# A graph-attention kernel on one core: q fetched as 32-bit rows instead of three bf16 parts

## The chip, the cores and the metric

The kernel runs on one core of one Trainium2 chip, in one launch. The metric is the device time of the whole program in microseconds (us); lower is better. The engines are named as in the profile: PE (TensorE, with its weight loads as PEld), DVE (VectorE), ACT (ScalarE), POOL (GpSimd) and SP (SyncE, which here only issues DMAs). The engines run their own instruction lists and meet only at semaphores, which the kernel sets and waits for by hand.

## What is computed

Two layers of a typed graph transformer over 6250 nodes and 100000 edges (sorted by destination), then a linear layer and a layer norm. One layer, cut to what matters:

```python
k = typed_linear(x, ntype, Wk); q = typed_linear(x, ntype, Wq); v = typed_linear(x, ntype, Wv)   # 6250 x 128
kT = einsum('nhd,htdo->nhto', k, Watt);  vT = einsum('nhd,htdo->nhto', v, Wmsg)                  # per node, 32 edge types
kw = kT[src, :, etype];  m = vT[src, :, etype]                                                   # 100000 rows, 8 heads x 16
a = einsum('ehd,ehd->eh', kw, q[dst]) * pri[:, etype].T / SQRT_D
att = edge_softmax(a, dst, n)
hag = segment_sum(m * att[:, :, None], dst)
h = silu(typed_linear(hag, ntype, Wa)) * alpha + x * (1 - alpha);  h = layernorm(h) * g + b
```

## The kernel before, in words

Each layer has two stages. `fused(l)` projects q, k and v node tile by node tile, builds the table of all (node, edge type) rows (kT and vT side by side, 256 words) and stores it to DRAM; the q rows go to DRAM in node order. `attend(l)` then walks over the edges. After the second layer `finish()` does the last layer norms and the output.

In `attend` the edges are laid out in slots of 128 edges; all edges of a slot have their destination in one tile of 128 nodes. Four slots are a quad, 8 quads a block (32 slots), and 26 blocks a layer, so that there are 208 quads in a layer and 416 in all. Blocks 0 and 1 are written out, the others run in a loop of six blocks per turn. For each quad:

- POOL (`gather`, L790 to L798) issues four indirect DMAs (L796), each fetching 128 table rows into one slot of `rows`, a ring of three blocks (24 quads). From the 25th quad on it first waits until PE has summed the quad that had the place (`sum_psum`). Each of the DMAs counts up the semaphore `rows_in` of the quad.
- SP (`load_places`, L607) loads the places of the quad's edges in their node tile, broadcast to all partitions, in bf16.
- DVE (`turned`, L1755 to L1761) compares them with the partition's number: one instruction makes `onehotT`, 128 nodes x 512 edges, of ones and zeros. It runs two quads ahead.
- PE (`fetch_q`, L1272 to L1282) multiplies `onehotT` with the q rows of the slot's node tile, which puts q[dst] for 128 edges into PSUM. It runs one quad ahead. q lies in SBUF as three bf16 parts (`q_parts`, high, middle and low) whose sum is the 32-bit number, so there are three products per slot that add up in PSUM, 12 per quad. Before them PE waits for `onehotT_ready` and for `prod_ready` of the quad before the last.
- DVE (`multiply`, L1748) multiplies PSUM with the gathered k rows, after `rows_in` and `q_psum`; `head_sums` (L1763, the reduce in L1766) adds them up per head; `find_maxima` does, spread over the next block's quads, the softmax maxima of a block.
- DVE (`weigh`, L1770, with its multiplication in L1775) weighs the messages 12 quads later, PE (`sum_quad`, L1284, its products in L1293) sums them per node with a second one-hot that ACT makes (`mark`, L1010, lines L1015 and L1018), and DVE (`add`, L1784, L1790) adds the sums to `sums` in SBUF.

The products of `sum_quad` have 32-bit operands on both sides; each stands in the trace as two loads and two products, so 8 records per quad; each of them has 136 columns.

Ahead of the first quad of each layer stands a start-up. SP loads q from DRAM into the space of `sums` in four parts (L629). ACT copies the upper halves of the 32-bit words as bf16 (L1042), DVE subtracts them (L1907), ACT copies the rest, DVE subtracts again, ACT copies the last rest: 12 copies and 8 subtractions, chained by `q_copied` and `q_left`. Only then does DVE clear `sums` (L1910), make the first two `onehotT`, and PE begin its first fetch (L1354). POOL's gathers do not wait for any of this, only for the table's last store.

Of the kernel before, what the change touches and what calls it, by code (L numbers as in the profile page):

```python
# [19 lines left out]
P = 128  # L20
N, E, D, H, HS, RT, NT, L = 6250, 100000, 128, 8, 16, 32, 16, 2
NTILES = -(-N // P)
# [15 lines left out]
CLEN = PER_CHUNK * P  # L38
QUAD = 4
# [9 lines left out]
ONEHOT_RING, DST_RING = 3, 4  # L49
# [31 lines left out]
def gnn_kernel(nc, x, src, dst, etype, ntype, Wk, Wq, Wv, Wa, Watt, Wmsg, pri, skip, ln_g, ln_b, ff_w, ff_b, out):  # L81
    F32, I32, BF16 = mybir.dt.float32, mybir.dt.int32, mybir.dt.bfloat16
    ALU, ACT, AX = mybir.AluOpType, mybir.ActivationFunctionType, mybir.AxisListType
# [3 lines left out]
    with ctx:  # L87
# [3 lines left out]
        def sem(name):  # L91
            return ctx.enter_context(nc.semaphore(name))
# [13 lines left out]
        q_dram = dram("q_rows", [NPAD, D], F32)  # L106
# [41 lines left out]
        q_parts = region_q[:, :].rearrange("p (c k d) -> p c k d", c=NTILES, k=3)  # L148
# [10 lines left out]
        q_stage = spare[:, 0:NTILES * D].rearrange("p (c d) -> p c d", c=NTILES)  # L159
# [14 lines left out]
        def take(whole, base, words, pattern, **sizes):  # L174
            return whole[:, base:base + words].rearrange(pattern, **sizes), base + words
# [44 lines left out]
        turned_words = arena[:, o + DST_RING * QUAD * P // 2:o + (DST_RING + 2) * QUAD * P // 2]  # L220
        onehotT = turned_words.bitcast(BF16).rearrange("p (r s e) -> p r s e", r=2, s=QUAD)
        flags, o = take(arena, o + (DST_RING + 2) * QUAD * P // 2, 4 * CLEN, "p (r k e) -> p r k e", r=2, k=2)
# [48 lines left out]
        q_copied, q_left = sem("q_copied"), sem("q_left")  # L271
# [199 lines left out]
        def _(sp):  # L471
# [127 lines left out]
            def attend(l):  # L599
# [28 lines left out]
                for k, part in enumerate(Q_PARTS):  # L628
                    sp.dma_start(q_stage[:, part], q_dram.rearrange("(c p) d -> p c d", p=P)[:, part]).then_inc(q_in[k], 16)  # L629
# [202 lines left out]
        def _(act):  # L832
# [176 lines left out]
            def attend(l):  # L1009
# [26 lines left out]
                for m in range(3):  # L1036
                    for k, part in enumerate(Q_PARTS):
                        if m == 0:
                            act.wait_ge(q_in[k], 16 * (l + 1))
                        else:  # L1040
                            act.wait_ge(q_left, 8 * l + 4 * m + k - 3)
                        nc.scalar.copy(q_parts[:, part, m], q_stage[:, part].bitcast(BF16)[:, :, 1::2]).then_inc(q_copied, 1)  # L1042
# [25 lines left out]
        def _(pe):  # L1068
# [196 lines left out]
            def attend(l):  # L1265
# [6 lines left out]
                def fetch_q(block_, q, tiles):  # L1272

                    quad = block_.quad(l, q)
                    pe.wait_ge(onehotT_ready, quad + 1)
                    wait(pe, prod_ready, quad - 1)
                    for s in range(QUAD):
                        for k in range(3):
                            ins = nc.tensor.matmul(bank[1 + q % 2][:, s * D:(s + 1) * D], onehotT[:, q % 2, s],  # L1279
                                                   q_parts[:, bass.ds(tiles[s], 1), k, :].rearrange("p a n -> p (a n)"),  # L1280
                                                   start=(k == 0), stop=(k == 2))
                    ins.then_inc(q_psum, 1)  # L1282
# [68 lines left out]
                pe.wait_ge(q_copied, 12 * (l + 1))  # L1351
# [20 lines left out]
        def _(dve):  # L1372
# [374 lines left out]
            def attend(l):  # L1747
# [156 lines left out]
                for m in range(2):  # L1904
                    for k, part in enumerate(Q_PARTS):
                        dve.wait_ge(q_copied, 12 * l + 4 * m + k + 1)
                        v.tensor_tensor(q_stage[:, part], q_stage[:, part], q_stage[:, part].bitcast(BF16)[:, :, 1::2],  # L1907
                                        ALU.subtract).then_inc(q_left, 1)
                dve.wait_ge(q_copied, 12 * (l + 1))
# [47 lines left out]
```

## Time and profile before

| | |
|---|---|
| median of three runs | 4279.86 us (4276.82 to 4286.49) |
| profiled execution: its time, its span | 4283.25 us, 4281.1 us |
| mean granted TensorE clock | 0.743 of full speed |
| busy: PE, DVE, ACT, POOL | 57%, 63%, 41%, 59% of the span |
| the fused stages | to about 640 us, and about 2020 to 2664 us |
| the attend stages | about 640 to 2021 us, and about 2664 to 4100 us |

A share of busy time is a mean over stages. Idle time of an engine is charged, in brackets or in a column of its own, to the event that ended it; "issue" means that the profile shows no event, and "remote" stands for a semaphore that came from a DMA or from elsewhere. A granted clock of 0.5 is 1.2 GHz, 1.0 is 2.4 GHz; a mean between them is a mixture in time. The profile shows q's part of `region_q` and `onehotT` under the names of the SBUF tensors that hold them (`region_q`, `arena`, `sums`, `region`).

### The profile page before, as it was taken

To read this page: it belongs to the slowest core of one execution; us is meant where nothing else is said; L and a number is where in the kernel's file an instruction comes from. 1 tells how busy PE (TensorE), PEld (TensorE's weight loads), DVE (VectorE), ACT (ScalarE), POOL (GpSimd) and SP (SyncE) were. 2 spreads that over 40 slices of the span, in tenths; PEclk is the share of its full clock that TensorE was granted. 3 is DMA by queue.
4 is the path that set the end of the run, shared out by engine and by line. 5 is a ranking of instruction groups with operands and counts; after the bars stand their busy time and mean duration, and the time that the engine had idled before them with its cause. 6 is when DMAs were issued, how large, how long until landed. Compare 5 with 4: busy or idle time off the path is not lost.

```text
span 4281.1 us, 61152 instructions
## 1 busy us (share of the span) xinstructions
PE 2425.5 (57%) x14449; PEld 1695.8 (40%) x14450; DVE 2687.2 (63%) x6722; ACT 1742.2 (41%) x3994; POOL 2538.0 (59%) x2596
## 2 busy tenths in 40 slices
PE   3777770455555555556677776055565555555365
PEld 1333330344444444445333332044444444444243
DVE  6666662566666666667678787156666566666466
ACT  3666661133332333334567666023323333332255
POOL 4666657466666666661566665746666666666426
PEclk8899885677767676777799888567777666767666
DMA  8999984344444444444799997334443434444131
GB/s 199 410 409 410 415 330 126 85 117 118 115 124 117 117 118 115 111 115 108 236 389 381 406 399 311 111 86 111 114 115 111 112 110 115 112 116 112 55 107 49
DMA packets 321852, 783.07 MB, mean 183 GB/s; under 512 B 87083, under 2 KB 249803, under 8 KB 309007
## 3 DMA queue, kind: packets, MB, share of 16 engines
q0 software_dynamic: 110672, 651.37, 42.8%
q1 hardware_dynamic: 202387, 127.10, 11.8%
q8 instruction: 152, 2.49, 0.2%
q10 hardware_dynamic: 8448, 0.53, 0.1%
q14 instruction: 193, 1.58, 0.1%
HBM read 335.58 MB, written 573.46 MB: 212 GB/s over the span
## 4 chain that ended last, share of the span: by engine, by line
DVE 19%; another core or an unknown queue 18%; issue 18%; PE 17%; DMA 16%; ACT 6%; DVEq 4%; POOL 3%; SPq 0%; ACTq 0%; POOLq 0%
DMA relation_table<-region,scatter_node 14%; PE bank L1293 6%; DVE sums L1790 6%; PE bank L1279 4%; ACT region L879 3%; PE bank L1124 2%; DVE region L1775 2%; DVEq L1779 2%; DVE region L1753 1%; DVEq L1790 1%; PE bank L1331 1%; ACT arena L1015 1%; DVE arena L1761 1%; PE bank L1154 1%
## 5 line engine op out<-in xcount | busy, mean ns | idle before, releaser
L796 POOL DMA_INDIRECT region<-relation_table,key_of x1664 | 1633.6, 982 | 980.5 <-issue 463.6
L1293 PE MATMUL bank<-region,arena 128*128 128x136 f32 x3328 | 732.0, 385 | 520.2 <-DVE region L1775 276.7
L1753 DVE TENSOR_TENSOR region<-bank,region 128x512 f32<-128x512 f32 x416 | 285.3, 686 | 1013.9 <-remote 780.9
L1015 ACT ACTIVATE arena<-iota_free,minus_dst 128x128 f32<-128x128 f32 x1664 | 529.0, 388 | 876.6 <-remote 578.6
L1293 PEld LDWEIGHTS bank<-region,arena 128*128 128x128 f32 x3328 | 627.4, 272 | 609.1 <-DVE sums L1790 285.9
L1279 PE MATMUL bank<-region_q,arena 128*128 x4992 | 573.2, 269 | 365.4 <-issue 273.1
L879 ACT COPY region<-bank 128x512 f32<-128x512 f32 x1152 | 623.6, 602 | 364.2 <-DMA relation_table<-region,scatter_node 225.8
L1124 PE MATMUL bank<-sums,arena 128*128 128x512 bf16 x2048 | 625.8, 414 | 254.2 <-ACT region L879 211.2
L1579 DVE COPY region<-bank 128x512 f32<-128x512 f32 x896 | 585.2, 685 | 269.1 <-DMA relation_table<-region,scatter_node 174.8
L1279 PEld LDWEIGHTS bank<-region_q,arena 128*128 128x128 bf16 x4992 | 481.1, 123 | 446.2 <-issue 395.6
L1790 DVE TENSOR_TENSOR sums<-sums,bank 128x136 f32 x1664 | 474.3, 285 | 76.9 <-DVE sums L1790 34.8
L1026 ACT ACTIVATE region<-arena 128x256 f32<-128x256 f32 x52 | 21.7, 417 | 1030.5 <-DVE arena L1859 901.9
L1124 PEld LDWEIGHTS bank<-sums,arena 128*128 128x128 bf16 x2048 | 194.3, 102 | 590.6 <-ACT region L879 287.8
L1775 DVE TENSOR_TENSOR region<-region 128x512 f32<-128x512 f32 x416 | 284.2, 684 | 2.2 <-issue 0.7
L1766 DVE TENSOR_REDUCE arena<-region 128x32 f32<-128x512 f32 x416 | 280.5, 674 | 0.2
L1018 ACT ACTIVATE arena<-arena 128x512 f32<-128x512 f32 x416 | 262.0, 630 | 13.1
L720 POOL TENSOR_TENSOR sums<-arena,sums 128x256 f32<-128x256 f32 x128 | 86.0, 672 | 260.7 <-ACT arena L897 258.7
L1586 DVE COPY arena<-bank 128x1024 bf16<-128x1024 bf16 x256 | 175.3, 685 | 42.5 <-PE bank L1145 17.8
L1331 PE MATMUL bank<-ident,arena 128*1 128x128 f32 x416 | 104.7, 409 | 127.6 <-DVE arena L1824 103.9
L1145 PE MATMUL bank<-identb,sums 128*128 128x128 bf16 x2048 | 173.5, 233 | 2.8 <-POOL sums L724 2.8
L1145 PEld LDWEIGHTS bank<-identb,sums 128*128 128x128 bf16 x2048 | 150.3, 105 | 53.9 <-issue 15.2
L737 POOL DMA_INDIRECT relation_table<-region,scatter_node x128 | 129.1, 1009 | 70.7 <-issue 35.9
(245 smaller groups left out, 2752.1 us busy)
## 6 DMA issues: line engine op xcount, KB each, us to landing
arena<-edge_places SPq DMA_DIRECT2D x416, 128.0 KB
region<-relation_table,key_of POOLq DMA_INDIRECT x1664
arena<-segment_flags SPq DMA_DIRECT2D x104, 128.0 KB
sums<-q_rows SPq DMA_DIRECT2D x6, 768.0 KB, 7.3
aggregated_rows<-one_less_alpha SPq DMA_DIRECT2D x17, 256.0 KB
region<-aggregated_rows SPq DMA_DIRECT2D x16, 272.0 KB, 3.1
sums<-relation_weight_parts SPq DMA_DIRECT2D x32, 128.0 KB
x_sorted<-arena SPq DMA_DIRECT2D x16, 256.0 KB
```

Source lines behind the costliest of these rows:

```text
L796: pool.indirect_dma_start(out=rows[:, block_.r, q * QUAD + s], out_offset=None, in_=table, in_offset=bass.IndirectOffsetOnAxis(ap=key_of[: ...
L879: nc.scalar.copy(stage[:, r, :, k * HS:(k + 1) * HS], bank[TABLE_BANK + k % TABLE_BANKS][:, :].rearrange("p (t o) -> p t o", t=RT)).then_i ...
L1015: chain.step(nc.scalar.activation(onehots[:, at, s], iota_free[:, :], ACT.Abs, bias=minus_dst[:, bass.ds(block_.b * BLOCK + (q * QUAD + s) ...
L1124: nc.tensor.matmul(bank[TABLE_BANK + k % TABLE_BANKS][:, :], x_spreadT[:, k, :], w_rel[:, k, :], start=True, stop=True).then_inc(table_psu ...
L1145: ins = nc.tensor.transpose(bank[SPREAD_BANK[half]][:, :].bitcast(BF16)[:, k * P:(k + 1) * P], x_spread[:, tile.par, half * H + k].rearran ...
L1279: ins = nc.tensor.matmul(bank[1 + q % 2][:, s * D:(s + 1) * D], onehotT[:, q % 2, s], q_parts[:, bass.ds(tiles[s], 1), k, :].rearrange("p ...
L1293: ins = nc.tensor.matmul(bank[SUM_BANK[q % 2][pair]][:, s * SUMC:(s + 1) * SUMC], onehots[:, at, 2 * pair + s], rows[:, block_.r, slot, RH ...
L1579: v.tensor_copy(stage[:, r, :, k * HS:(k + 1) * HS], bank[TABLE_BANK + k % TABLE_BANKS][:, :].rearrange("p (t o) -> p t o", t=RT)).then_in ...
L1753: v.tensor_tensor(here, bank[1 + q % 2][:, :].rearrange("p (s d) -> p s d", s=QUAD), here, ALU.mult).then_inc(prod_ready, 1)
L1766: v.tensor_reduce(score[:, block_.par, q * QUAD:(q + 1) * QUAD, :], rows[:, block_.r, q * QUAD:(q + 1) * QUAD, 0:D].rearrange("p s (h o) - ...
L1775: v.tensor_tensor(msg, msg, bc(part[:, :, RHS0:D], 3, HS), ALU.mult).then_inc(weighted, 1)
L1790: v.tensor_tensor(total, total, bank[SUM_BANK[q % 2][n // 2]][:, (n % 2) * SUMC:(n % 2 + 1) * SUMC], ALU.add).then_inc(sum_added, 1)
```

## The change

q stays in SBUF as it comes from DRAM: 32-bit rows, in the space in which the three parts lay. `onehotT` becomes a 32-bit tensor, lies behind them, and each slot has one product. The 12 copies of ACT, the 8 subtractions of DVE and their two semaphores go. PE waits for the four loads of q itself, DVE for the last product of the table (the space of `sums` is free then) before it clears `sums`.

```diff
-        q_parts = region_q[:, :].rearrange("p (c k d) -> p c k d", c=NTILES, k=3)
-        q_stage = spare[:, 0:NTILES * D].rearrange("p (c d) -> p c d", c=NTILES)
+        q_rows = wqf[:, 0:NTILES * D].rearrange("p (c d) -> p c d", c=NTILES)
+        onehotT = wqf[:, NTILES * D:NTILES * D + 2 * QUAD * P].rearrange("p (r s e) -> p r s e", r=2, s=QUAD)
...
-        turned_words = arena[:, o + DST_RING * QUAD * P // 2:o + (DST_RING + 2) * QUAD * P // 2]
-        onehotT = turned_words.bitcast(BF16).rearrange("p (r s e) -> p r s e", r=2, s=QUAD)
...
-                    sp.dma_start(q_stage[:, part], q_dram.rearrange("(c p) d -> p c d", p=P)[:, part]).then_inc(q_in[k], 16)
+                    sp.dma_start(q_rows[:, part], q_dram.rearrange("(c p) d -> p c d", p=P)[:, part]).then_inc(q_in[k], 16)
...
-                for m in range(3):
-                    for k, part in enumerate(Q_PARTS):
-                        if m == 0:
-                            act.wait_ge(q_in[k], 16 * (l + 1))
-                        else:
-                            act.wait_ge(q_left, 8 * l + 4 * m + k - 3)
-                        nc.scalar.copy(q_parts[:, part, m], q_stage[:, part].bitcast(BF16)[:, :, 1::2]).then_inc(q_copied, 1)
...
-                        for k in range(3):
-                            ins = nc.tensor.matmul(bank[1 + q % 2][:, s * D:(s + 1) * D], onehotT[:, q % 2, s],
-                                                   q_parts[:, bass.ds(tiles[s], 1), k, :].rearrange("p a n -> p (a n)"),
-                                                   start=(k == 0), stop=(k == 2))
+                        ins = nc.tensor.matmul(bank[1 + q % 2][:, s * D:(s + 1) * D], onehotT[:, q % 2, s],
+                                               q_rows[:, bass.ds(tiles[s], 1), :].rearrange("p a n -> p (a n)"), start=True, stop=True)
...
-                pe.wait_ge(q_copied, 12 * (l + 1))
+                for k in range(len(Q_PARTS)):
+                    pe.wait_ge(q_in[k], 16 * (l + 1))
...
-                for m in range(2):
-                    for k, part in enumerate(Q_PARTS):
-                        dve.wait_ge(q_copied, 12 * l + 4 * m + k + 1)
-                        v.tensor_tensor(q_stage[:, part], q_stage[:, part], q_stage[:, part].bitcast(BF16)[:, :, 1::2],
-                                        ALU.subtract).then_inc(q_left, 1)
-                dve.wait_ge(q_copied, 12 * (l + 1))
+                dve.wait_ge(table_psum, 2 * H * TILES * (l + 1))
                 link(v.memset(sums[:, :, :], 0.0))
```

## Rows read from the trace of the kernel before

**Rows 1.** Windows: PE, PEld, DVE, ACT, POOL busy us; clock; DMA share; GB/s.

```profile
850.00:1940.00 1090.00, 602.72 (x3913) 502.31 (x3914) 685.73 (x1947) 341.84 (x927) 690.03 (x704) 0.71 0.43 116
1945.00:2020.00 75.00, 54.30 (x316) 45.82 (x315) 62.63 (x185) 40.45 (x111) 0.04 (x1) 0.70 0.42 108
```

**Rows 2.** Waits of DVE and POOL, 850 to 1940: us, times, longest.

```profile
DVE region L1753 <- remote: 255.6, 58, 10.4
DVE region L1753 <- PE bank L1279: 78.8, 21, 10.2
...
POOL region L796 <- remote: 144.5, 59, 3.2
POOL region L796 <- PE bank L1293: 62.1, 43, 2.8
```

**Rows 3.** Timeline of layer 0's start-up: start, us, engine, what, idle before.

```profile
661.98 5.61 DVE L1910 MEMSET sums<- 128x6664 f32 x1 [3.92 <-issue]
...
668.12 1.77 PE L1279 MATMUL bank<-region_q,arena 128*128 x12 [34.22 <-issue]
...
766.71 0.95 POOL L796 DMA_INDIRECT region<-relation_table,key_of  x1 [0.30 <-issue]
781.21 0.69 DVE L1753 TENSOR_TENSOR region<-bank,region 128x512 f32<-128x512 f32 x1 [16.60 <-remote]
```

**Rows 4.** The same in layer 1.

```profile
2790.93 0.95 POOL L796 DMA_INDIRECT region<-relation_table,key_of  x1 [0.30 <-issue]
...
2805.37 0.69 DVE L1753 TENSOR_TENSOR region<-bank,region 128x512 f32<-128x512 f32 x1 [14.60 <-remote]
```

**Rows 5.** Groups, POOL from 642 to 672: busy us, mean ns, idle before.

```profile
L796 POOL DMA_INDIRECT region<-relation_table,key_of x20 | 23.9, 1197 | 12.3 <-DMA relation_table<-region,scatter_node 6.5 <-issue 5.8
```

**Rows 6.** Groups over the whole span, same columns.

```profile
L796 POOL DMA_INDIRECT region<-relation_table,key_of x1664 | 1633.6, 982 | 980.5 <-issue 463.6 <-remote 306.4 <-PE bank L1293 197.2
L1293 PE MATMUL bank<-region,arena 128*128 128x136 f32 x3328 | 732.0, 385 | 520.2 <-DVE region L1775 276.7 <-issue 93.9 <-ACT arena L1018 76.5
...
L1279 PE MATMUL bank<-region_q,arena 128*128 x4992 | 573.2, 269 | 365.4 <-issue 273.1 <-DVE region L1753 59.2 <-DVE arena L1761 31.4
...
L1761 DVE TENSOR_SCALAR arena<-arena,row_no 128x512 bf16<-128x512 bf16 x416 | 150.6, 363 | 0.7 <-issue 0.6
```

**Rows 7.** Timeline of PE, a quad at either clock level.

```profile
1664.69 2.18 PE L1293 MATMUL bank<-region,arena 128*128 128x136 f32 x8 [6.64 <-DVE region L1775]
1666.66 1.46 PE L1279 MATMUL bank<-region_q,arena 128*128 x12
...
1941.76 1.19 PE L1293 MATMUL bank<-region,arena 128*128 128x136 f32 x8 [0.31 <-issue]
1942.79 0.83 PE L1279 MATMUL bank<-region_q,arena 128*128 x12
```

**Rows 8.** Groups, two compares in 32 bits on DVE in the preparation.

```profile
L1511 DVE TENSOR_SCALAR region<-region_q 128x896 f32<-128x896 f32 x1 | 0.7, 686 | 0.0
...
L1406 DVE TENSOR_SCALAR ident<-iota_free,region 128x128 f32<-128x128 f32 x1 | 0.3, 280 | 0.0
```

**Rows 9.** Windows, L796 alone: busy us (gathers), clock, DMA share, GB/s.

```profile
3560.00:3660.00 100.00, 63.76 (x65) 0.66 0.41 113
3660.00:3760.00 100.00, 64.17 (x64) 0.73 0.42 113
...
3860.00:3960.00 100.00, 64.39 (x67) 0.76 0.42 115
```

**Rows 10.** Timelines of DVE and POOL, two gathers beside DVE work.

```profile
1605.19 0.68 DVE L1775 TENSOR_TENSOR region<-region 128x512 f32<-128x512 f32 x1
1605.23 1.47 POOL L796 DMA_INDIRECT region<-relation_table,key_of  x1 [0.30 <-issue]
...
1612.35 0.94 POOL L796 DMA_INDIRECT region<-relation_table,key_of  x1 [1.90 <-PE bank L1293]
...
1612.54 0.35 DVE L1761 TENSOR_SCALAR arena<-arena,row_no 128x512 bf16<-128x512 bf16 x1
```

More of the change, by code:

```diff
@@ L219, in gnn_kernel @@
         edge_places = places_words.bitcast(BF16).rearrange("p (r e) -> p r e", r=DST_RING)
-        turned_words = arena[:, o + DST_RING * QUAD * P // 2:o + (DST_RING + 2) * QUAD * P // 2]
-        onehotT = turned_words.bitcast(BF16).rearrange("p (r s e) -> p r s e", r=2, s=QUAD)
-        flags, o = take(arena, o + (DST_RING + 2) * QUAD * P // 2, 4 * CLEN, "p (r k e) -> p r k e", r=2, k=2)
+        flags, o = take(arena, o + DST_RING * QUAD * P // 2, 4 * CLEN, "p (r k e) -> p r k e", r=2, k=2)
         carry_in = sb("carry_in", [1, 2, 2, H, CHUNKS + 1], F32)
@@ L270, in gnn_kernel @@
         q_in = [sem(f"q_in{i}") for i in range(4)]
-        q_copied, q_left = sem("q_copied"), sem("q_left")
         table_psum, stage_act, stage_dve = sem("table_psum"), sem("stage_act"), sem("stage_dve")
```

## The prediction

> **What bounds the kernel now.** I read the busy time by stretch first. In 1090 us of layer 0's attend stage 704 gathers are issued, 176 quads, so a quad takes 6.19 us; DVE is busy 63% of that, PE 55%, POOL 63%, the DMA engines 43% [rows 1]. No engine is full. Then what they wait for: DVE stands before `multiply` (L1753) for 255.6 us because of "remote", and for 78.8 us because of the q fetch [rows 2]. POOL issues a gather every 0.95 + 0.30 = 1.25 us when nothing holds it [rows 3], 5.0 us a quad; the missing 1.2 us are its waits, 144.5 + 62.1 = 206.6 us over 176 quads [rows 2]. So POOL and DVE take turns in waiting, with a ring of 24 quads between them. Once POOL has issued its last gather, DVE is busy 62.63 of 75 us and runs 84% full [rows 1]: DVE and PE alone are faster than 6.19 us a quad, and something that goes with the gathers holds them back.
>
> The start of a layer shows this best. POOL issues the 96 gathers of the ring in one stream, the last at 766.71, and DVE, which did its first multiplication soon after the first fetch at 668.12, comes to its fifth only at 781.21, 13.6 us after the end of the last gather [rows 3]. In layer 1 it is 2790.93 + 0.95 and 2805.37, 13.5 us [rows 4]. The profile does not say what DVE waits for there (it calls it remote), but the release is tied to POOL's stream and not to when PE and DVE began.
>
> The sum is made against the profiled execution (4283.25 us, span 4281.1); the median of the runs is 3.4 us lower, and I take that off at the end.
>
> **The start-up.** Twelve copies and eight subtractions go, which end just before the clearing at 661.98. PE was idle for 34.22 us before 668.12, so the table's last product ended at 633.90 [rows 3], and the clearing (5.61) can begin there, 28 us earlier, beside the loads of q. The first `onehotT` and the first fetch can't be earlier than 639.5; q and the places have still to be loaded, so I put the fetch at about 650, 18 us earlier. What hides this: POOL's stream. It sets the release at 781.21 [rows 3], so 18 us of head start buy nothing, except that POOL's first gathers were held up by the subtractions: 20 gathers took 23.9 us instead of 20 x 0.95 = 19.0 [rows 5]. 4.9 us a layer come off; bounds 0 and, if the head start counts, 18 more (a rival). The waits that are added (PE for the q loads, DVE for the table's last product) are met before: SP's loads wait for that product too. Behind DVE's wait stand the clearing and the first `onehotT`, for which PE's first fetch waits. SP's queue keeps its four loads and its order, POOL's too. Together: -10 us.
>
> The Trainium skill, page SBUF — State Buffer, section Who interferes with whom, says that DVE and GpSimd share one port pair as a lock, taken by a DVE instruction with two SBUF inputs or in a two-port mode. This agrees with the slow gathers beside the subtractions [rows 5].
>
> **PE, the fetch.** 12 bf16 products a quad (1.38 us: 573.2 us over 416 quads) become 4 products of 32 bits. Their cost stands in the trace: `sum_quad`'s are of the same kind with 136 columns, 732.0 us for the same number of slots; with 128 columns 689.0 us, 1.66 us a quad [rows 6]. So +0.28 us a quad. By clock level it is 2.18 x 128/136 = 2.05 against 1.46 at 1.2 GHz and 1.12 against 0.83 at 2.4 GHz [rows 7], so +0.59 at the most; at the least -0.6, if the time goes by records (12 in 1.77 us at the first fetch [rows 3], 8 would take 1.18). I take 0.28, the mean of all.
>
> **DVE, `turned`.** 512 elements in bf16 take 0.363 us [rows 6]; the output is 32 bits wide now. Two compares in 32 bits took 0.280 us for 128 and 0.686 for 896 elements, 0.53 ns an element, which gives 0.48 us for 512 [rows 8]: +0.12 us. Bounds 0, and +0.32 if it runs as L1775 does (0.68 for 512 [rows 10]).
>
> A rule speaks against the change here. The Trainium skill, page VectorE: DVE Perf Modes, section The perf-mode tier table, lets a tensor_scalar run four elements a cycle when all is bf16 in SBUF and two in fp32, 693 against 1227 ns for 2048 elements. By it 512 elements would cost 0.13 us more (an estimate, a quarter of the difference) in place of 0.12. No row here has a bf16 input with a 32-bit output.
>
> **What the quad pays.** The two make 0.40 us a quad on engines that wait for more than that: DVE for 255.6/176 = 1.45 us [rows 2]. How much comes through can be read where PE's speed changes by itself. Between clock 0.66 and 0.76 PE has 20 points more of its time at the upper level; a sum and a fetch differ by 0.99 + 0.63 us between the levels [rows 7], so PE saves 0.32 us a quad. The gathers in 100 us are 65 and 67, but 64 at 0.73 [rows 9]: a quad is shorter by 0.18 us or longer by 0.1. So between 0.56 and nothing comes through. I take 0.1, near the lower end, as three windows show no order: 0.40 x 0.1 x 352 quads of both layers = +14 us; bounds 0 and 0.56 x (0.59 + 0.32) x 352 = +179.
>
> Some fetches are drawn out, and DVE waits 78.8 us a layer for them [rows 2]. With 8 records for 12 a third may go, 53 us in both layers, of which the same 0.1 to 0.56 comes through: -5 to -29, I take -10.
>
> **Where POOL is quiet** nothing hides the extra work. After 781.21 nine quads are multiplied before the first sum lets POOL go on, at the lower clock: 0.59 + 0.12 each, half of it side by side, 3 us. At the end about eleven quads are multiplied after the last gather: 0.12 + half of 0.28 each, 3 us. For both layers +12 us.
>
> Sum: -10 + 14 - 10 + 12 = +6 on 4283.25, minus 3.4 for the runs: 4286; with the first multiplications of a layer perhaps one quad further by the release (1 us each) **4284 us**. The bounds of PE's and DVE's extra work give 4262 to 4305 for this case.
>
> **The rivals.** *The extra work comes through (slower).* Place: the ring's turn from `multiply` through `weigh` and `sum_quad` to POOL's next gather. If 0.56 of the 0.40 us comes through instead of 0.1, it costs 79 us in place of 14: 4284 + 65 = 4349. For it: 62.1 us in which POOL waits for L1293 [rows 2], the pair 65 and 67 [rows 9]. Against it: the 64. It decides from about 0.15 on.
>
> *The head start counts (faster).* If DVE's release follows its own first multiplication and not POOL's stream, 18 us come off each layer: 4284 - 36 = 4248. For it: PE stands idle for 34.22 us before its first fetch [rows 3]. Against it: 13.6 and 13.5 us after POOL's end in both layers [rows 3, 4].
>
> *The fetch was the brake (faster).* If DVE's waits for L1279 halve and come through in full, 79 us go in place of 10, and 4284 - 69 = 4215. For it: 365.4 us of idle before L1279, 273.1 of them without a releaser [rows 6]; against it: only 21 waits in 1090 us [rows 2].
>
> *The gathers are stretched (slower).* POOL's gathers last 0.982 us on average, 0.95 when alone, 0.13 us a quad too long [rows 6, 3]. If `turned` did that and lasts 0.12/0.363 = 33% longer, 0.04 us a quad come on POOL's own time: +15 us, 4299. Against it: the gather at 1612.35 lies beside a `turned` and lasts 0.94, the one at 1605.23 beside L1775 and lasts 1.47 [rows 10].
>
> By the SBUF rule of the Trainium skill cited above both instructions can take the shared pair; the rows show it for L1775 alone.
>
> **How the numbers follow.** About 0.2% (8.6 us) is what a measurement of this kernel can tell from no change. The likeliest case (4284, its own range 4262 to 4305) gets 0.46, of which 0.28 lies within 0.2% of 4279.86, 0.13 above and 0.05 below. The slower rival gets 0.18, the stretched gathers 0.08, the head start 0.17, the fetch as brake 0.11. Faster 0.05 + 0.17 + 0.11 = 0.33, same 0.28, slower 0.13 + 0.18 + 0.08 = 0.39. The range takes in the head start, and the slower rival for the most part: 4240 to 4345.
>
> **What the profile after would show.** Right: the first fetch near 650 and 2674, DVE's fifth multiplication still 13 to 14 us after the ring's last gather and some 5 us earlier than before; the fetch as 8 records a quad with about 690 us of PE; `turned` near 0.48 us; 64 to 67 gathers in 100 us, DVE's remote wait shorter by about what DVE and PE gained in work. Wrong: a release that moved by 15 us or more, fewer than 64 gathers in 100 us, `turned` at 0.65 us or more, or fetch records well over 0.25 us each at the lower clock.

## The result and the profile after

The changed kernel takes 4220.13 us (median of four runs, 4214.90 to 4224.53), the kernel before beside it 4283.17: ratio 0.9857, 95% interval 0.9844 to 0.9871. It is 61 us faster. I had forecast 4284 and a range of 4240 to 4345.

The first line of either page gives the span and the number of recorded instructions, of the kernel before and of the changed one:

```profile
span 4281.1 us, 61152 instructions
```

```profile
span 4222.7 us, 54460 instructions
```

The stretch from 850 to 1900 us, in which both kernels gather in layer 0 (PE, PEld, DVE, ACT, POOL busy us; clock; DMA share; GB/s), before and after:

```profile
850.00:1900.00 1050.00, 583.16 (x3775) 485.71 (x3776) 660.43 (x1877) 333.85 (x906) 665.23 (x679) 0.71 0.43 116
```

```profile
850.00:1900.00 1050.00, 605.09 (x3143) 532.84 (x3143) 692.66 (x1903) 332.96 (x902) 679.14 (x692) 0.73 0.42 118
```

PE and DVE do more work, as forecast, and yet POOL gets 692 instructions in, nearly all of them gathers, where it got 679: a quad takes 6.07 us instead of 6.19. The waits of DVE and POOL in the same stretch, before and after:

```profile
DVE region L1753 <- remote: 244.7, 56, 10.4
DVE region L1753 <- PE bank L1279: 76.2, 20, 10.2
...
POOL region L796 <- remote: 136.9, 56, 3.2
```

```profile
DVE region L1742 <- remote: 237.9, 61, 9.9
DVE region L1742 <- PE bank L1268: 57.6, 26, 5.6
...
POOL region L793 <- remote: 120.6, 49, 3.2
```

In this stretch DVE waits 6.8 us less for "remote" and 18.6 less for the fetch, POOL 16.3 less for "remote". In layer 1 (2870 to 3900 us) it is 50.3 less, 2.1 less and 36.8 less. The groups (busy us, mean ns, idle before):

```profile
L793 POOL DMA_INDIRECT region<-relation_table,key_of x1664 | 1630.6, 980 | 926.8 <-issue 465.4 <-remote 241.9 <-PE bank L1281 208.3
...
L1268 PE MATMUL bank<-region_q 128*128 x3328 | 620.6, 349 | 240.1 <-DVE region L1742 117.3 <-issue 102.2 <-DVE region_q L1750 19.6
...
L1750 DVE TENSOR_SCALAR region_q<-arena,row_no 128x512 f32<-128x512 bf16 x416 | 204.7, 492 | 13.8 <-issue 7.0 <-DMA arena<-edge_places 6.7
```

`turned` came out as worked out from [rows 8], 0.49 us (forecast 0.48). The fetch takes 620.6 us of PE, 47 more than before [rows 6], where 116 more were forecast. The start-up, first in the kernel before (rows between those of [rows 3]), then in the changed one:

```profile
696.34 0.69 DVE L1753 TENSOR_TENSOR region<-bank,region 128x512 f32<-128x512 f32 x1 [23.73 <-remote]
729.38 0.69 DVE L1753 TENSOR_TENSOR region<-bank,region 128x512 f32<-128x512 f32 x1 [31.49 <-issue]
762.98 0.69 DVE L1753 TENSOR_TENSOR region<-bank,region 128x512 f32<-128x512 f32 x1 [32.05 <-remote]
```

```profile
647.07 5.44 PE L1268 MATMUL bank<-region_q 128*128 x24 [13.95 <-issue]
...
719.14 0.69 DVE L1742 TENSOR_TENSOR region<-bank,region 128x512 f32<-128x512 f32 x1 [20.72 <-remote]
...
741.54 0.69 DVE L1742 TENSOR_TENSOR region<-bank,region 128x512 f32<-128x512 f32 x1 [20.59 <-remote]
...
760.59 0.95 POOL L793 DMA_INDIRECT region<-relation_table,key_of  x1 [0.30 <-issue]
763.94 0.69 DVE L1742 TENSOR_TENSOR region<-bank,region 128x512 f32<-128x512 f32 x1 [20.72 <-remote]
775.84 0.69 DVE L1742 TENSOR_TENSOR region<-bank,region 128x512 f32<-128x512 f32 x1 [10.22 <-remote]
```

DVE is let go at 775.84, 14.3 us after the end of POOL's last gather of the ring (760.59 + 0.95): tied to POOL's stream, as forecast, and 5.4 us earlier. But this is its ninth multiplication; the fifth, for which I had named that moment, comes at 696.74. By the release it has multiplied eight quads, not four. While POOL issues without a pause, quads are taken up 22.40 us apart (741.54 - 719.14), in the kernel before 33.60 us (762.98 - 729.38). Nothing that I had forecast makes that difference, and it became the measure of most experiments. POOL's 25th quad starts 155.2 us after its first one, before it was 165.1.

The starts of the gathers say where the 61 us come from. From a layer's first gather to its 25th quad it is 10 us less in either layer (155.2 and 155.8 in place of 165.1 and 165.3). From there to the last gather a quad takes 6.08 us in both layers in place of 6.18 and 6.16, which is 19 and 16 us less over 184 quads. Together that is 55 of the 58 us between the two profiled executions.

### The profile page after: what moved, and what is told of

It is laid out like the page before. It is cut to its first block, busy times and chain, and to the rows that moved or that the text cites. A ratio compares the mean times of both kernels' runs of the same rounds, so it can differ in the third digit from the quotient of the medians.

```text
span 4222.7 us, 54460 instructions
## 1 busy us (share of the span) xinstructions
PE 2457.1 (58%) x12785; PEld 1801.8 (43%) x12786; DVE 2713.9 (64%) x6706; ACT 1710.2 (40%) x3970; POOL 2537.3 (60%) x2596
## 4 chain that ended last, share of the span: by engine, by line
DVE 19%; PE 18%; issue 18%; another core or an unknown queue 17%; DMA 16%; ACT 4%; DVEq 4%; POOL 3%; SPq 0%; POOLq 0%; ACTq 0%
DMA relation_table<-region,scatter_node 14%; PE bank L1281 7%; DVE sums L1779 6%; PE bank L1268 4%; PE bank L1114 3%; ACT region L876 2%; DVE region L1764 1%; DVEq L1768 1%; DVE region L1742 1%; DVEq L1779 1%; DVE region_q L1750 1%; PE bank L1144 1%; DVE region L1568 1%; PE bank L1319 1%
## 5 line engine op out<-in xcount | busy, mean ns | idle before, releaser
L1281 PE MATMUL bank<-region,arena 128*128 128x136 f32 x3328 | 708.9, 377 | 548.7 <-DVE region L1764 270.2
L1281 PEld LDWEIGHTS bank<-region,arena 128*128 128x128 f32 x3328 | 613.3, 267 | 631.1 <-DVE sums L1779 311.5
L1742 DVE TENSOR_TENSOR region<-bank,region 128x512 f32<-128x512 f32 x416 | 285.1, 685 | 895.8 <-remote 659.0
L1268 PE MATMUL bank<-region_q 128*128 x3328 | 620.6, 349 | 240.1 <-DVE region L1742 117.3
L1268 PEld LDWEIGHTS bank<-region_q 128*128 128x128 f32 x3328 | 585.9, 263 | 252.8 <-issue 252.1
L1750 DVE TENSOR_SCALAR region_q<-arena,row_no 128x512 f32<-128x512 bf16 x416 | 204.7, 492 | 13.8 <-issue 7.0
```

Of the source, the lines that this page charges most:

```text
L1281: ins = nc.tensor.matmul(bank[SUM_BANK[q % 2][pair]][:, s * SUMC:(s + 1) * SUMC], onehots[:, at, 2 * pair + s], rows[:, block_.r, slot, RH ...
L1742: v.tensor_tensor(here, bank[1 + q % 2][:, :].rearrange("p (s d) -> p s d", s=QUAD), here, ALU.mult).then_inc(prod_ready, 1)
```

## The experiments

Each group of four (the last of two) ran on one chip with the kernel before beside it; the groups ran on different chips. "Pace" is the time from one quad's multiplication to the next in layer 0's start-up, while POOL streams. A "pair" is one weight load and one product of PE.

**The short start-up alone** (e1):

```diff
-                for m in range(3):
+                for m in range(1):
...
-                                                   q_parts[:, bass.ds(tiles[s], 1), k, :].rearrange("p a n -> p (a n)"),
+                                                   q_parts[:, bass.ds(tiles[s], 1), 0, :].rearrange("p a n -> p (a n)"),
```

(The subtractions go too, and the waits are for four copies a layer.)

> The kernel before with only the start-up shortened: ACT makes the high bf16 part alone (4 copies a layer, no subtraction), and all three products of a slot read that part, so the fetch keeps its 12 products, register-addressed as before; q is fetched without its middle and low parts. Theory A (the number of PE's products sets the pace at which quads are taken up while POOL streams, and a part of the steady pace): the first fetch comes about 18 us earlier, POOL's stream ends about 5 us earlier, quads in the stream stay 33 us apart, the steady quad stays at 6.19 us: about 16 us less in all, 4267, ratio 0.996. Theory B (the head start is the whole gain): ratio 0.986. My prediction's own reading: 10 us less, 4273, ratio 0.9977.

Measured: 4255.67 us, ratio 0.9933 (0.9917 to 0.9950), 28 us less; pace 33.6. The text above is wrong in one thing: the kernel records 57792 instructions, 3360 fewer than the one before. Where three products read the same address one register operation serves all three, so this edit took away 8 of 12 register operations a quad as well. Two later kernels pull the two apart.

**One product per slot** (e2): `for k in range(3)` becomes `for k in range(1)` on top of e1.

> As the kernel with the short start-up, but one bf16 product per slot in place of three (q without its middle and low parts): 4 products a quad, PE's fetch about 0.5 us a quad, no 32-bit operand and no slower onehotT. Theory A (fewer products): quads in POOL's stream 22 us apart as in the changed kernel, steady quad 6.08 us or less, total 4205 to 4220, ratio 0.982 to 0.986. Rival C (the 32-bit form itself gives the gain): as the short start-up alone, about 4267, ratio 0.996. Rival D (it is PE's busy time that counts): 0.9 us less PE work a quad gives more than the change did, below 4190.

Measured: 4165.75 us, ratio 0.9728 (0.9712 to 0.9745), 118 us less than before and 54 less than the changed kernel. Rows of DVE while POOL streams:

```profile
690.98 0.69 DVE L1753 TENSOR_TENSOR region<-bank,region 128x512 f32<-128x512 f32 x1 [8.77 <-remote]
702.18 0.69 DVE L1753 TENSOR_TENSOR region<-bank,region 128x512 f32<-128x512 f32 x1 [9.65 <-remote]
```

The pace is 11.20 us (single quads take 10.50 to 11.90). Rival C falls: the 32-bit form is not needed for the gain.

**Fixed tiles for two of three products** (e3), on top of e1:

```diff
+                                                   q_parts[:, bass.ds(tiles[s], 1) if k == 0 else slice(s, s + 1), 0, :]
```

> As the kernel with the short start-up, 12 bf16 products a quad, but only one product of each slot takes its tile from a register; the other two read a fixed tile (other data, same size). So 12 products and 4 register operations a quad in place of 12 and 12. If the register operations are the brake (theory A1): like the kernel with one product, ratio about 0.984. If the products and weight loads themselves are (theory A2): like the short start-up alone, ratio 0.996, quads in the stream 33 us apart. In between if both count.

Measured: 4258.34 us, ratio 0.9936 (0.9917 to 0.9955), as e1. As e1 already had 4 register operations, it only says that the address doesn't matter.

**The 32-bit products cut in two** (e4):

```diff
+                        for h in range(2):
+                            ins = nc.tensor.matmul(bank[1 + q % 2][:, s * D + h * 64:s * D + (h + 1) * 64], onehotT[:, q % 2, s],
+                                                   q_rows[:, bass.ds(tiles[s], 1), h * 64:(h + 1) * 64].rearrange("p a n -> p (a n)"), start=True, stop=True)
```

> The changed kernel with each 32-bit product cut into two of 64 columns: 8 products and 8 register operations a quad in place of 4 and 4, the same columns, the same result. Theory A: quads in the stream 26 to 30 us apart in place of 22.3, the steady quad about 0.05 us longer, total 4240, ratio 0.990. If the count does not matter: 4220, ratio 0.986, and PE's extra work alone (4 more weight loads of 32 bits a quad, about 0.8 us) tells what PE's work costs.

Measured: 4344.47 us, ratio 1.0140 (1.0123 to 1.0157), 124 us over the changed kernel, more than any theory gave. The half products last as long as whole ones (0.351 us each in place of 0.349), so the fetch takes 1175.1 us of PE in place of 620.6, and the 124 us are not the number's alone. The pace:

```profile
711.07 0.69 DVE L1743 TENSOR_TENSOR region<-bank,region 128x512 f32<-128x512 f32 x1 [42.34 <-issue]
755.87 0.69 DVE L1743 TENSOR_TENSOR region<-bank,region 128x512 f32<-128x512 f32 x1 [43.12 <-issue]
```

With 4, 8, 12 and 16 pairs of load and product in the trace the pace is 11.20, 22.40, 33.60 and 44.80 us: 2.80 us for each pair, with nothing left over.

**Two bf16 products a slot** (e5): as e2 with `range(2)`.

> The kernel with the short start-up and two bf16 products a slot (both with the high part; q without its middle and low parts): 8 products and weight loads a quad, as many as the 32-bit form leaves in the trace, but less PE time (0.27 us each instead of 0.35 and no slower onehotT). Theory R (the number of PE's weight loads and products counts, not their time): quads in POOL's stream 22.4 us apart, steady quad about 6.08 us, total about 4215 to 4225, ratio 0.985. Theory T (PE's busy time counts): halfway between one and three products, quads in the stream not at 22.4, total about 4205 if T alone, below the changed kernel by 10 us or more.

Measured: 4214.62 us, ratio 0.9842 (0.9826 to 0.9859).

```profile
715.53 0.69 DVE L1753 TENSOR_TENSOR region<-bank,region 128x512 f32<-128x512 f32 x1 [20.86 <-issue]
737.93 0.69 DVE L1753 TENSOR_TENSOR region<-bank,region 128x512 f32<-128x512 f32 x1 [20.85 <-issue]
```

As many pairs as the changed kernel, the same pace of 22.40, and nearly its time, with 374.8 us of PE in the fetch instead of 620.6.

**Small products in place of large ones** (e6), on top of e2:

```diff
+                        for k in range(2):
+                            nc.tensor.matmul(bank[1 + q % 2][:, s * D + k:s * D + k + 1], onehotT[:, q % 2, s],
+                                             q_parts[:, s, 0, k:k + 1], start=True, stop=True)
```

> The kernel with one bf16 product a slot and, ahead of each, two products of a single column that the real one overwrites (the same one-hot, a fixed place of q): 12 weight loads and products a quad, with the PE time of little more than four; q without its middle and low parts. Theory R (count): quads in the stream 33.5 us apart, total near 4255, ratio 0.993. Theory T (time): about 4175, ratio 0.975, quads in the stream near 11 us apart.

Measured: 4248.17 us, ratio 0.9917 (0.9900 to 0.9933), pace 33.59 us:

```profile
716.94 0.69 DVE L1756 TENSOR_TENSOR region<-bank,region 128x512 f32<-128x512 f32 x1 [32.14 <-issue]
750.53 0.69 DVE L1756 TENSOR_TENSOR region<-bank,region 128x512 f32<-128x512 f32 x1 [31.98 <-remote]
```

Eight products of one column cost as much as eight of 128. For the pace the number counts, not the columns. Over the whole kernel this run tells less: the small products take 0.185 us each, and the fetch has 598.6 us of PE, more than the 494.9 of e1. It is e5 beside the changed kernel that sets the number against PE's time.

**Small copies on DVE** (e7), on top of e2, in `head_sums`:

```diff
+                    for n in range(8):
+                        v.tensor_copy(probe[:, n:n + 1], row_no[:, 0:1])
```

> The kernel with one bf16 product a slot (q without its middle and low parts) and eight copies of one column a quad on DVE, ahead of head_sums. If any instruction counts, whatever its engine (theory R2): as with 8 more products, 33 us apart in the stream and near 4255, ratio 0.993. If only PE's records count: quads in the stream stay 11 us apart, and the total goes up only by the part of DVE's extra time (8 times 0.07 us a quad) that comes through, 0 to 0.56 us on 352 quads, 4166 to 4300, near 4190.

Measured: 4217.47 us, ratio 0.9854 (0.9837 to 0.9870), about 54 us more than e2 by the ratios; pace 15.40 us. Here are DVE's rows of one such quad:

```profile
718.77 0.69 DVE L1754 TENSOR_TENSOR region<-bank,region 128x512 f32<-128x512 f32 x1
720.86 0.35 DVE L1762 TENSOR_SCALAR arena<-arena,row_no 128x512 bf16<-128x512 bf16 x1 [1.40 <-issue]
728.59 0.46 DVE L1768 COPY probe<-row_no 128x1 f32<-128x1 f32 x6 [7.37 <-remote]
729.96 0.15 DVE L1768 COPY probe<-row_no 128x1 f32<-128x1 f32 x1 [0.92 <-issue]
732.06 0.15 DVE L1768 COPY probe<-row_no 128x1 f32<-128x1 f32 x1 [1.95 <-issue]
733.46 0.69 DVE L1769 TENSOR_REDUCE arena<-region 128x32 f32<-128x512 f32 x1 [1.25 <-issue]
734.17 0.69 DVE L1754 TENSOR_TENSOR region<-bank,region 128x512 f32<-128x512 f32 x1
```

DVE's instructions count too. There are two ways to read by how much. Eight copies add 4.20 us to e2's pace, half a us each. Or the engine with the most instructions sets the pace: DVE has 11 in this quad (multiplication, `turned`, eight copies, reduce), and 11 x 1.40 = 15.40; PE's loads and products, 8, 16, 24 and 32 a quad in the kernels above, give 11.20, 22.40, 33.60 and 44.80 at the same 1.40 us for one. The next run speaks for the second. The copies have 0.58 us of DVE a quad themselves, so the 54 us are not the number's alone.

**One more compare** (e8), on the changed kernel:

```diff
+                    v.tensor_scalar(second[:, q % 2], edge_places[:, q % DST_RING], row_no[:, 0:1], None, ALU.is_equal)
                     v.tensor_scalar(flat, edge_places[:, q % DST_RING], row_no[:, 0:1], None, ALU.is_equal).then_inc(onehotT_ready, 1)
```

> The changed kernel with the compare of turned made twice, the first into space that nobody reads: 0.48 us of DVE work a quad more, nothing else. It asks how much of DVE's extra work comes through. My prediction took 0.1 of it (0.05 us a quad, about 18 us: 4238, ratio 0.9895); its slower rival took 0.56 (0.27 us a quad, 95 us: 4315, ratio 1.007).

Measured: 4236.53 us, ratio 0.9894 (0.9877 to 0.9910), 16 us over the changed kernel by the ratios, which are uncertain by some 8 us from chip to chip. A tenth of DVE's time gives as much. The pace did not move:

```profile
699.88 0.69 DVE L1743 TENSOR_TENSOR region<-bank,region 128x512 f32<-128x512 f32 x1 [20.17 <-remote]
722.28 0.69 DVE L1743 TENSOR_TENSOR region<-bank,region 128x512 f32<-128x512 f32 x1 [20.21 <-remote]
```

Here DVE has four instructions a quad and PE 16 loads and products. At half a us for one more DVE instruction the pace would be 22.9 us; it is 22.40, 16 x 1.40.

**Short start-up with 12 register operations** (e9): on top of e1 the products of a slot read `0, k:D` and write `D - k` columns, so that each has an address of its own.

> The kernel with the short start-up alone had only 4 register operations a quad, since its three products of a slot read the same place. Here they start at column 0, 1 and 2 of the high part, with 128, 127 and 126 columns, each overwriting the last: 12 products and 12 register operations a quad, the short start-up. If the register operations cost nothing: as the kernel with the short start-up (4256, ratio 0.9933), and the head start is worth 28 us. If they do: the head start is the difference of this kernel to the one before, and the register operations the difference to 4256; my prediction's start-up of 10 us gives 4273, ratio 0.9977.

Measured: 4304.69 us, ratio 0.9984 (0.9971 to 0.9997), on a chip on which the kernel before took 4308.36. The pace is 33.59 us (762.27 - 728.68), as in e1: 12 or 4 register operations make no difference to it.

**POOL kept four quads ahead at the start** (e10), on the changed kernel:

```diff
+                    if block_.known and block_.b < DEPTH and (block_.b or q >= 4):
+                        pool.wait_ge(prod_ready, block_.quad(l, q) - 3)
```

> The changed kernel, where POOL in the first 24 quads of a layer waits until the multiplication of the quad four before is done, so that it never issues its gathers in one stream. Theory R (PE's and DVE's work is taken up slowly only while POOL issues without a pause): quads are multiplied 7 to 8 us apart from the start in place of 22.4, and the 25th quad's gather starts later than now (155.5 us after the first) by 10 to 25 us, most of it given back by sums already done: total 4225 to 4265. Rival (PE's products are slow at the start for another reason, loads of q and places, the clock): they stay 22 us apart, POOL is held to that, and a layer becomes over 300 us longer.

Measured: 4211.89 us, ratio 0.9775 (0.9759 to 0.9792). The timeline of POOL and DVE at the first pause:

```profile
676.53 0.95 POOL L795 DMA_INDIRECT region<-relation_table,key_of  x1 [0.30 <-issue]
682.05 0.69 DVE L1744 TENSOR_TENSOR region<-bank,region 128x512 f32<-128x512 f32 x1 [14.98 <-remote]
683.53 0.95 POOL L795 DMA_INDIRECT region<-relation_table,key_of  x1 [6.05 <-DVE region L1744]
683.65 0.68 DVE L1744 TENSOR_TENSOR region<-bank,region 128x512 f32<-128x512 f32 x1
...
685.46 0.69 DVE L1744 TENSOR_TENSOR region<-bank,region 128x512 f32<-128x512 f32 x1
...
687.16 0.69 DVE L1744 TENSOR_TENSOR region<-bank,region 128x512 f32<-128x512 f32 x1
```

POOL stops at 677.48; 4.6 us later DVE goes on and multiplies four quads within 5.1 us. The 25th quad starts 140.7 us after the first, 14.5 earlier than in the changed kernel (15.4 in layer 1), where I had expected it later. POOL's pause is what lets the others through, and giving it early pays. By ratio e10 is 35 us below the changed kernel, by microseconds 8, as the kernel before is 25 us slower on this chip; the two earlier 25th quads alone make 30.

**The sums in bf16** (e11 on the changed kernel, e12 on e2): second one-hot, exp and weighted messages are written in bf16, `sum_quad` reads them so.

```diff
+                    v.tensor_tensor(part16[:, :, H:SUMC].rearrange("p s (h o) -> p s h o", h=H), msg, bc(part16[:, :, 0:H], 3, HS), ALU.mult).then_inc(weighted, 1)
```

> The changed kernel with the products of sum_quad in bf16 (weighted messages, weights and the second one-hot rounded to bf16): 4 loads and products a quad for sums in place of 8, about 1.1 us of PE time less. Theory R (each load and product of PE costs 0.02 to 0.04 us a quad wherever it stands): 4 records less are worth 0.08 to 0.15 us a quad, total 4160 to 4185, ratio 0.972 to 0.978. If only the fetch counts, since only the fetch stands between DVE's multiplications: no change at all, 4220; if the sum's length counts too, for which POOL waits: below 4160.

> The kernel with one bf16 product a slot (q in bf16, short start-up) and the products of sum_quad in bf16 as well: 4 + 4 loads and products a quad in place of 12 + 8 of the kernel before. Theory R: from 4166 down by the same as the other run's step, 4100 to 4130, ratio 0.958 to 0.965. If the quad has reached POOL's own 5.0 us and its fixed wait, less.

Measured: 4210.52 us, ratio 0.9771 (0.9753 to 0.9789), and 4163.36, ratio 0.9659 (0.9641 to 0.9676). In microseconds they stand at their bases (4220 and 4166), which ran on other chips; by ratio they are 0.7 to 0.9% below. Since the kernel before was 25 us slower on this chip, I can't tell which is the fair comparison, and the step stays open.

**The same kernels once more, on one chip.**

> The changed kernel once more, beside the next two on one chip. Ratio 0.9857 as before; 0.7 to 0.8% below the kernel with the short start-up and 4 register operations a quad.

> The kernel with the short start-up, 12 products and 4 register operations a quad, once more. Ratio 0.9933 if its first measurement holds on another chip.

> The kernel with the short start-up, 12 products and 12 register operations a quad, once more, now beside the one with 4. If register operations cost time: ratio 0.998, 20 us (0.5%) over e14. If the difference came from the chips: the same as e14, 0.993.

> The kernel with one bf16 product a slot (q in bf16, short start-up), where POOL waits in the first 24 quads for the multiplication of the quad four before. If both gains add up: 0.9728 less 2 times 10 us for the 25th quad's earlier gather (143.9 us after the first one now, 133 to 140 then): 4145 to 4160, ratio 0.968 to 0.971. If the start-up has nothing left to give with four products: 0.973.

Measured: the kernel before 3708.97 us (31 runs, 3699.59 to 3720.56); e13 3714.53, ratio 1.0015 (1.0002 to 1.0027); e14 3700.42, 0.9983 (0.9973 to 0.9993); e15 3701.53, 0.9979 (0.9969 to 0.9988); e16 3701.83, 0.9977 (0.9966 to 0.9988). The expected ratios of e13, e14 and e16 did not come out. That of e15 (0.998) did, but not the 20 us over e14: it is 1 us. On this chip the same program is 570 us faster, and the change makes it 0.15% slower. Here are the window of e13 (columns as above), and POOL's and DVE's waits in it:

```profile
850.00:1650.00 800.00, 529.48 (x2824) 463.53 (x2824) 621.84 (x1700) 298.27 (x812) 611.42 (x619) 0.78 0.50 139
```

```profile
POOL region L793 <- issue: 186.7, 613, 0.3
POOL region L793 <- PE bank L1281: 1.8, 6, 0.3
...
DVE region L1742 <- DMA region<-relation_table,key_of: 147.1, 119, 3.1
```

The "remote" wait of DVE and POOL is gone. DVE waits for the gathers themselves, POOL for nothing: 619 gathers in 800 us are 5.17 us a quad, which is four times 0.988 + 0.30 us. While POOL streams, DVE follows it quad by quad:

```profile
691.78 0.69 DVE L1742 TENSOR_TENSOR region<-bank,region 128x512 f32<-128x512 f32 x1 [3.42 <-DMA region<-relation_table,key_of]
697.18 0.69 DVE L1742 TENSOR_TENSOR region<-bank,region 128x512 f32<-128x512 f32 x1 [2.20 <-DMA region<-relation_table,key_of]
```

What is left of the change is on POOL. The gathers' group of e13 and of e14, and a `turned` of each with the gather beside it:

```profile
L793 POOL DMA_INDIRECT region<-relation_table,key_of x1664 | 1644.3, 988 | 517.6 <-issue 502.7 <-DMA relation_table<-region,scatter_node 11.2 <-PE bank L1281 3.7
...
687.28 0.48 DVE L1750 TENSOR_SCALAR region_q<-arena,row_no 128x512 f32<-128x512 bf16 x1
687.38 1.20 POOL L793 DMA_INDIRECT region<-relation_table,key_of  x1 [0.30 <-issue]
```

```profile
L796 POOL DMA_INDIRECT region<-relation_table,key_of x1664 | 1630.0, 980 | 519.1 <-issue 504.2 <-DMA relation_table<-region,scatter_node 12.8 <-PE bank L1293 2.1
...
683.49 0.37 DVE L1761 TENSOR_SCALAR arena<-arena,row_no 128x512 bf16<-128x512 bf16 x1
683.53 0.95 POOL L796 DMA_INDIRECT region<-relation_table,key_of  x1 [0.30 <-issue]
```

The gathers take 1644.3 - 1630.0 = 14.3 us more, POOL's idle time before them is the same within 2 us, and the kernel takes 14.1 us more. e15 and e16, whose `turned` writes bf16 too, have gathers of 1628.8 and 1628.1 us and times of 3701.53 and 3701.83. Of some 1600 gathers in either trace, 454 of e13 overlap a `turned` and last 0.987 us on average, 414 of e14 do and last 0.963; an undisturbed one lasts 0.947. That is 18 us over in e13 and 7 in e14, most of the difference. `turned` is the cause that fits; no run changes its output alone.

**Register operations alone** (e17), on the kernel before: only the `q_parts` line of e1's diff.

> The kernel before, start-up and all, but its three products of a slot read the high part (q without its middle and low parts), so that one register operation serves all three: 4 register operations a quad in place of 12, 3300 recorded instructions fewer, nothing else. Count theory, on a chip where the kernel before takes about 4280 us: 3300 times 11.5 ns, 38 us less, ratio 0.991 (0.993 to 0.995 if the 20 us read between the other two kernels holds). If register operations cost nothing: 1.000. On a chip where the kernel before takes about 3709 us: 1.000 in either case.

The kernel before took 4285.61 us on this chip. Measured: 4263.57 us, ratio 0.9951 (0.9937 to 0.9965), with 57824 recorded instructions. The pace stays where it was:

```profile
730.50 0.69 DVE L1753 TENSOR_TENSOR region<-bank,region 128x512 f32<-128x512 f32 x1 [31.50 <-issue]
764.10 0.69 DVE L1753 TENSOR_TENSOR region<-bank,region 128x512 f32<-128x512 f32 x1 [32.05 <-remote]
```

So the 21 us do not come by the way of the pace. The fetch also takes less of PE's time with it, 500.9 us in place of 573.2, and this run doesn't say which of the two, the number or the time, they come from.

**Small copies on ACT** (e18), on the changed kernel, in `mark`:

```diff
+                    for n in range(8):
+                        nc.scalar.copy(probe[:, n:n + 1], row_no[:, 0:1])
```

> The changed kernel with eight copies of one column a quad on ACT, in the middle of mark: 3328 recorded instructions more on an engine that is busy 41% and waits at every quad. Count theory, on a chip where the kernel before takes about 4280 us: 3328 times 11.5 ns, 38 us more than the changed kernel's 4220, ratio 0.9945. If only PE's and DVE's instructions count: 0.9857, 4220. On a chip with 3709 us: as the changed kernel there, 1.0015, unless ACT's extra time (8 times 0.2 us a quad) reaches the path.

Measured, on the same chip: 4238.11 us, ratio 0.9886 (0.9870 to 0.9903), 12 us over the changed kernel where one price for every instruction gave 38. The rule that all instructions count alike falls: 3328 on ACT cost 12 us, as many of PE in e5 against e1 39.

## Why the prediction was wrong

The ratios on the chips where the kernel before takes about 4280 us split the change into parts (in us of 4280; each step starts from the kernel of the step above, so that they add up by construction):

| part | from | us | forecast |
|---|---|---|---|
| 8 of 12 register operations a quad go | e17 | -21 | none named |
| the short start-up | e1 against e17 (0.9933, 0.9951) | -8 | -10 |
| 8 pairs of load and product in place of 12 | e5 against e1 (0.9842, 0.9933) | -39 | -10 |
| 32-bit products, wider `turned` | changed kernel against e5 (0.9857, 0.9842) | +6 | +14, and +12 where POOL is quiet |
| sum | | -62 | +6 |

Each difference of two ratios from different chips is uncertain by some 0.2%, 8 us, so the third part is sure and the split of the two small ones is not.

- **The start-up** was right in size and mechanism. The gathers beside the old subtractions went from 1.197 us [rows 5] to 0.96, the release stayed tied to POOL's stream in both layers (14.3 us behind it), and the head start, 21 us in the end (647.07 in place of 668.12), bought nothing that shows. e9 (0.9984) and e15 (0.9979) are this step alone: 7 and 8 us. The sign that I had named, the fifth multiplication, did not come, for the reason in the third point.
- **The cost of the work** was right in kind and somewhat too high: `turned` 0.49 us as forecast, the fetch 0.11 us a quad longer instead of 0.28, and about a tenth of DVE's time comes through (e8: 16 us, forecast 18). The case's own range, 4262 to 4305, doesn't follow from its terms: with PE's lower bound of -0.6 us a quad they reach down to 4249 at the least. It changes nothing here.
- **The step that failed is the pricing of the fetch by PE's time, with the "drawn-out fetches" as the only place where fewer instructions could pay.** I gave it -10 us, a fifth of a third of DVE's waits for L1279; the instructions that went are worth -60. Most of the gain did not come through that wait but through the one the profile calls "remote", for DVE 780.9 us over the span before and 659.0 after, for POOL 306.4 and 241.9. I had read it as a tie to the gathers alone. On these chips each load and each product of the fetch takes 1.40 us of the pace while POOL streams, whatever its size. Over the whole kernel e2, e5 and e1 give 49 and 39 us for four pairs a quad, some 0.1 us a quad.
- **The rival "the fetch was the brake"** named nearly the right time (4215), but mostly by the wrong wait, and that is luck: DVE's wait for L1279 went from 162.6 to 147.3 us over the span, not by half.
- **The rival "the gathers are stretched"** (+15 us) fits what was measured. On the chip where POOL alone sets the pace it is the 14 us between e13 and e14, and the start-up's 8 us against it leave the 6 us (0.15%) by which the change is slower there. I had argued against it from one gather beside a bf16 `turned` [rows 10], which says nothing of one that writes 32 bits.
- **Open:** what is shared by POOL's stream and the other engines' instructions on most of these chips and not on one. The trace shows no event for it. The paces measured are 1.40 us for each instruction of the engine that has most of them in a quad (8, 11, 16, 24 and 32), as of something that takes them one by one at a fixed rate while POOL streams. The 11 stand for one run only (e7), and ACT has no instruction of e18's in the stream. Register operations are recorded too, and 12 in place of 4 leave the pace at 33.6 (before and e9 against e1 and e17); so it is not a rate for every instruction that an engine gets, and the 21 us of e17 are not explained by it. Every timed run here carries the records of its instructions, so no run shows whether the recording itself takes part. The Trainium skill, page NOTIFIC — the notification-queue block, section 7.1 Overflow: three behaviours, one of which stalls the engine, describes such a path: inside the block, the records pass through a pipeline that holds up rather than loses one. No run here shows that it is this path.

By ratio the fastest kernel of all, q in bf16 and sums in bf16 (e12, 0.9659), and the simpler e2 (0.9728) beat both kernels, at the price of q's lower bits and, in e12, of the messages'. With everything in 32 bits the changed kernel with POOL's early pauses (e10, 0.9775) is the best measured. All three ran on chips where the effect is there; on the one without it no kernel is more than 0.23% under the one before.

## What to carry to other kernels

Price an edit by the number of instructions it takes away as well as by their time, above all where an engine waits for "remote" while another issues DMAs without a pause. Read the pace in such a stretch: it shows in two lines what a mean over the kernel hides. An instruction more costs there on the engine that has the most. And measure on more than one chip before a gain of a per cent is called a property of the kernel.

## What the hardware showed that I had not expected

- While POOL issues gathers in one stream, a quad takes DVE and PE 1.40 us for every load or product that PE has in the fetch (11.20, 22.40, 33.60, 44.80 us for 4, 8, 12, 16 pairs). With 11 instructions on DVE against 8 on PE it is 15.40 us, which fits 1.40 us for each on the engine with the most; one more on an engine with fewer (e8) leaves it at 22.40.
- A pause of POOL sets them free: 4.6 us after POOL's last gather in e10 (677.48, in the first quads), 14.3 us after it where the stream had lasted 120 us (761.54 in the changed kernel).
- One chip showed none of this: 3709 us for the kernel before where the others take 4281 to 4308.
- Three products that read the same register-addressed operand need one register operation, not three (e17 records 57824 instructions, the kernel before 61152: 8 a quad); with them 21 us and 72 us of PE's time in the fetch went, on the chip without the effect (e14 against e15) 1 us.
- A compare that reads bf16 and writes 32 bits can slow a gather that starts beside it (1.20 in place of 0.95 us); beside one that writes bf16 the gather lasted 0.95. The Trainium skill, page SBUF — State Buffer, section Who interferes with whom, lets a tensor_scalar in a two-port mode lock GpSimd out of the shared pair. The row of e13 agrees for the compare that writes 32 bits; the row of e14 shows no lock for the one that writes bf16.
